# A recommender layer on one core: fields in five groups of four and three of two, and 22 weight loads halved

## The reference, cut to what matters

```python
sparse_embed = emb_tables[field_idx[None, :], x_sparse]      # 512 x 26 x 64
z = sparse_embed.reshape(B, N_FIELDS * K)
gram = jnp.einsum('bik,bjk->bij', sparse_embed, sparse_embed)
inner = gram[:, iu, ju]                                       # i < j
dnn_in = jnp.concatenate([x_dense, z, inner], axis=-1)        # 512 x 2002
h = jax.nn.relu(dnn_in @ w1 + b1)                             # w1: 2002 x 2002
out = jax.nn.sigmoid(h @ w2 + b2)
```

## Time and profile before

| | |
|---|---|
| median of the runs | 206.7 us |
| the profiled execution's own time | 207.33 us |
| its span, first to last instruction | 205.5 us |
| TensorE (PE) matmul, busy | 197.4 us (96%) |
| TensorE weight load (PEld), busy | 162.1 us |
| VectorE (DVE), busy | 145.1 us |
| ScalarE (ACT), busy | 129.9 us |
| GpSimd (POOL), busy | 125.0 us |
| mean granted TensorE clock | 0.988 of 2.4 GHz |

### The profile page before, as it was taken

One profiled execution on the slowest core, in us unless ns is written; L12 is line 12 of the kernel. 1 busy time (PEld: TensorE's weight loads), 2 busy tenths in 40 slices (PEclk: granted clock), 3 DMA queues, 4 the chain that ended last, 5 costly groups with the idle time before them and its releaser, 6 DMA issues.

```text
span 205.5 us, 3833 instructions
## 1 busy us (share of the span) xinstructions
PE 197.4 (96%) x1332; PEld 162.1 (79%) x1332; DVE 145.1 (71%) x342; ACT 129.9 (63%) x261; POOL 125.0 (61%) x169
## 2 busy tenths in 40 slices
PE   8994999999999999999999999999999999999993
PEld 8953888888888887887888888888888887788882
DVE  3574929696859769589874999688487787563573
ACT  2683627586958779687378755877699946632101
POOL 4777778778777783818988989889890000052000
PEclk9999799999999999999999999999999999999998
DMA  5579887676678589334599548988786185043000
GB/s 142 127 268 271 259 273 230 181 237 202 215 214 307 199 255 308 62 107 104 183 329 358 154 119 257 322 245 256 244 290 227 19 299 190 3 54 64 20 0 0
DMA packets 15206, 39.01 MB, mean 190 GB/s; under 512 B 3975, under 2 KB 5051, under 8 KB 15187
## 3 DMA queue, kind: packets, MB, share of 16 engines
q1 hardware_dynamic: 11250, 34.92, 52.1%
q0 software_dynamic: 3584, 3.76, 9.2%
q10 hardware_dynamic: 353, 0.08, 0.2%
HBM read 37.71 MB, written 0.69 MB: 187 GB/s over the span
## 4 chain that ended last, share of the span: by engine, by line
PE 85%; DVE 5%; POOL 4%; DMA 3%; issue 2%; ACT 0%; DVEq 0%
PE slot L1112 25%; PE slot L1115 24%; PE slot L1118 24%; PE slot L1072 5%; POOL E L843 4%; DMA E<-emb,row_idx 2%; PE slot L1102 2%; PE slot L1104 2%; PE slot L1103 2%; DVE w_lo L962 2%; DVE G L1010 1%; DMA x_idx<-idx 1%; DVE slot L1036 1%; DVE x_lo L992 0%; DVE T L979 0%
## 5 line engine op out<-in xcount | busy, mean ns | idle before, releaser
L843 POOL DMA_INDIRECT E<-emb,row_idx x104 | 110.9, 1067 | 33.3 <-issue 23.4
L962 DVE TENSOR_TENSOR w_lo<-w_raw,w_hi 128x500 fp32r<-128x500 f32 (+5 forms) x128 | 80.4, 671 | 11.8 <-ACT w_hi L880 11.6
L880 ACT CAST w_hi<-w_raw 128x1000 fp32r<-128x1000 f32 (+5 forms) x64 | 65.0, 1030 | 20.2 <-DMA w_raw<-w 11.8
L1112 PE MATMUL slot<-w_hi,x_hi 128*128 128x500 f32 (+5 forms) x236 | 74.9, 399 | 2.9 <-ACT x_hi L906 2.8
L1115 PE MATMUL slot<-w_lo,x_hi 128*128 128x500 f32 (+5 forms) x236 | 73.9, 394 | 0.1
L1118 PE MATMUL slot<-w_hi,x_lo 128*128 128x500 f32 (+5 forms) x236 | 73.1, 391 | 0.0
L1112 PEld LDWEIGHTS slot<-w_hi,x_hi 128*128 128x128 f32 (+2 forms) x236 | 43.9, 190 | 12.9 <-ACT x_hi L906 3.7
L1115 PEld LDWEIGHTS slot<-w_lo,x_hi 128*128 128x128 f32 (+2 forms) x236 | 45.0, 191 | 9.9 <-DVE w_lo L962 0.7
L1118 PEld LDWEIGHTS slot<-w_hi,x_lo 128*128 128x128 f32 (+2 forms) x236 | 44.9, 190 | 9.3
L911 ACT COPY ET<-T 32x128 f32<-32x128 f32 (+4 forms) x89 | 32.1, 360 | 2.1
L979 DVE STREAM_TRANSPOSE T<-E 128x256 f32<-128x256 f32 x24 | 10.6, 442 | 16.9 <-DMA E<-emb,row_idx 16.9
(11 more groups left out here) (42 smaller groups left out, 85.6 us busy)
## 6 DMA issues: line engine op xcount, KB each, us to landing
w_raw<-w SPq DMA_DIRECT2D x32, 501.0 KB, 4.8
w_raw<-w SPq DMA_DIRECT2D x32, 500.0 KB, 4.8
E<-emb,row_idx POOLq DMA_INDIRECT x104, 4.1
w_all<-w SPq DMA_DIRECT2D x1, 1001.0 KB, 4.5
gram_dram<-G SPq DMA_DIRECT2D x6, 84.5 KB
x_in<-gram_dram SPq DMA_DIRECT2D x6, 42.0 KB
x_in<-G SPq DMA_DIRECT2D x3, 58.5 KB
gram_dram<-G POOLq DMA_DIRECT2D x2, 84.5 KB, 5.3
```

Source lines behind the costliest of these rows:

```text
L843: nc.gpsimd.indirect_dma_start(out=E[:, k % ER, j, :], out_offset=None, in_=emb_rows, in_offset=bass.IndirectOffsetOnAxis(ap=row_idx[:, at ...
L880: nc.scalar.copy(w_parts(m)[0], w_source(m)).then_inc(w_hi_ready, 1)
L962: nc.vector.tensor_tensor(lo[:, cols], w_source(m)[:, cols], hi[:, cols].bitcast(F32), ALU.subtract)\
L1112: nc.tensor.matmul(acc[q], xh, hi[:, cols[q]], start=first, stop=False)
```

## The change

The 26 fields are now five groups of four (`WIDE`) and three of two (`NARROW`). In stage A the three narrow groups come first (`ORDER_A`), for batch tiles 0 and 1 in turn; in stage B they come last (`ORDER_B`). Each narrow group has its own place in X24; the intermediate T6 is shared by turns. Loads 4 to 25 (`HALVED`) are issued as two DMAs of 64 rows each, the first after gather `GATE[m]`, the second after gather `GATE[m] + 1`. `GATE` for m = 4, 5, 6 goes from 6, 7, 8 to 7, 9, 10. The two matmuls of `KEEP` are gone. `HELD_BACK` moves by one arrival, since two more arrivals come in A, and some assumed durations of the planner change.

```diff
-GROUP_GATHERS = [4] * WIDE + [2]
-GROUP_ORDER = [LAST] + list(range(WIDE))
+WIDE, NARROW = 5, 3
+GROUP_GATHERS = [4] * WIDE + [2] * NARROW
+ORDER_A = list(range(WIDE, GROUPS_Z)) + list(range(WIDE))
+ORDER_B = list(range(GROUPS_Z))
+ARRIVALS = ([(bt, g) for g in ORDER_A[:-2] for bt in (0, 1)] + [(bt, g) for bt in (0, 1) for g in ORDER_A[-2:]]
+            + [(bt, g) for g in ORDER_B for bt in (2, 3)])
...
-GATE = {2: 3, 3: 3, 4: 6, 5: 7, 6: 8, 7: 11, 8: 12, 9: 13, 10: 15, 11: 16, 12: 19, 13: 20, 14: 23, 15: 24, 16: 27, 17: 28,
+GATE = {2: 3, 3: 3, 4: 7, 5: 9, 6: 10, 7: 11, 8: 12, 9: 13, 10: 15, 11: 16, 12: 19, 13: 20, 14: 23, 15: 24, 16: 27, 17: 28,
         18: 31, 19: 32, 20: 35, 21: 36, 22: 39, 23: 40, 24: 41, 25: 43, 26: 50}
+HALVED = range(4, 26)
-KEEP_AT, KEEP = 3, 1
-HELD_BACK = {16: 2, 17: 4}
+HELD_BACK = {17: 2, 18: 4}
...
-ET_PARTS = [(LAST, LAST + 1), (0, 3), (3, 5), (5, 6)]
+ET_PARTS = [(WIDE, GROUPS_Z), (0, 2), (2, 4), (4, 5)]
...
-DVE_LEN = {"lo": 0.70, "turn": 0.46, "x24": 0.60, "x_lo": 0.44, "evac": 0.38, "park": 0.70, "drain": 0.86}
+DVE_LEN = {"lo": 0.70, "turn": 0.46, "x24": 0.50, "x_lo": 0.44, "evac": 0.38, "park": 0.70, "drain": 0.86}
-LAND = (1.7, 1.5, 1.1, 1.2) + (1.5,) * 10 + (4.5,)
+LAND = (1.7, 1.5, 1.5, 1.5) + (1.5,) * 12 + (4.5,)
...
-                    if m in GATE:
-                        sp.wait_ge(paced, paced_count(GATE[m]))
                     if m >= RAW:
                         sp.wait_ge(w_split, 2 * (m - RAW + 1))
-
-                    sp.dma_start(w_raw[:, m % RAW, 0:HALF_W[h]], w1[t, :, HALF_AT[h]:HALF_AT[h] + HALF_W[h]])\
-                      .then_inc(w_landed[m % RAW], 16)
+                    for n, rows in enumerate(load_rows(m)):
+                        if m in GATE:
+                            sp.wait_ge(paced, paced_count(GATE[m] + n))
+                        sp.dma_start(w_raw[rows, m % RAW, 0:HALF_W[h]], w1[t, rows, HALF_AT[h]:HALF_AT[h] + HALF_W[h]])\
+                          .then_inc(w_landed[m % RAW], 16)
...
+def load_rows(m):
+
+    return [slice(0, 64), slice(64, P)] if m in HALVED else [slice(0, P)]
...
             for step in PE_OPS:
-                if k == KEEP_AT and step[0] == "product":
-                    for n in range(KEEP):
-                        nc.tensor.matmul(slot[SLOT[cell_at(step)]][:, 0:BANK].rearrange("p (a b) -> p a b", a=4), ones[:],
-                                         ones[:].unsqueeze(1).to_broadcast([P, 4, P]), start=True, stop=True)
```

More of the change, by code:

```diff
@@ L159, in make_todo @@
     todo += [s for steps in later for s in steps[1:]]
-    first = [b_group("B1", 1, g) for g in GROUP_ORDER[:2]]
+    first = [b_group("B1", 1, g) for g in ORDER_B[:2]]
     todo += [s for bt in (2, 3) for f in first for s in f if s[2] == bt]
-    for n, g in enumerate(GROUP_ORDER[2:]):
+    for n, g in enumerate(ORDER_B[2:]):
         todo += b_group("B1", 1, g)
-        todo += b_group("B2", 0, GROUP_ORDER[n]) if n < 4 else []
-    rest = [s for g in GROUP_ORDER[4:] for s in b_group("B2", 0, g)]
+        todo += b_group("B2", 0, ORDER_B[n]) if n < 3 else []
+    rest = [s for s in b_group("B2", 0, ORDER_B[3])]
+    rest += [s for g in ORDER_B[4:] for s in b_group("B2", 0, g)]
+    todo, rest = todo + rest[:2], rest[2:]
     todo += mixed(rest[:7], gram({2, 3}), every=2) + rest[7:]
@@ L216, in length @@
         return 0.19 + 0.11 * n if engine == "act" else 0.16 + 0.11 * n
-    if op[0] in ("x_hi", "x_lo") and op[2] in [LAST] + INNER_KEYS:
+    if op[0] in ("x_hi", "x_lo") and op[2] >= WIDE:
         return 0.32
+    if op[0] == "turn" and ARRIVALS[op[1]][1] >= WIDE:
+        return 0.34
     if op[0] == "drain" and op[1][2] == "inner":
@@ L302, in et_ops @@
     def et_ops(bt, parts=range(len(ET_PARTS))):
-        return [("et", bt, p, i, h, v) for p in parts for i in range(2 if ET_PARTS[p][0] == LAST else 4) for h in (0, 1)
+        return [("et", bt, p, i, h, v) for p in parts for i in range(2 if ET_PARTS[p][0] == WIDE else 4) for h in (0, 1)
                 for v in ((0, 1) if bt in SPLIT else (None,))]
@@ L349, in update @@
             free = all_done(et_ops(bt - 2, [part_of(g)])) if bt >= 2 else 0.0
+            if g >= WIDE and (bt, g) in NARROWS[2:]:
+                back = NARROWS[NARROWS.index((bt, g)) - 2]
+                copied = all_done([("x24",) + back + (e,) for e in ("act", "dve")])
+                free = None if None in (free, copied) else max(free, copied)
             if free is not None:
@@ L443, in wanted @@
         if kind in ("turn", "x24", "x_hi", "x_lo"):
-            key = ARRIVALS[op[1]] if kind == "turn" else (op[1], LAST) if kind == "x24" else op[1:]
-            tail = {"turn": 2.1 if key[1] == LAST else 1.1, "x24": 1.3, "x_hi": 0.6, "x_lo": -0.3}[kind]
+            key = ARRIVALS[op[1]] if kind == "turn" else op[1:]
+            tail = {"turn": 1.7 if WIDE <= key[1] < IN_KEY else 1.1, "x24": 1.3, "x_hi": 0.6, "x_lo": -0.3}[kind]
             at = step_at(keys[key], tail)
@@ L484, in run @@
             if op + (other,) in done:
-                offer("act", ("x_hi", op[1], LAST), max(end, done[op + (other,)]) + HOP)
+                offer("act", ("x_hi",) + op[1:], max(end, done[op + (other,)]) + HOP)
         elif kind == "park":
@@ L490, in run @@
             bt, g = ARRIVALS[op[1]]
[L491 to L493 removed]
+            if g >= WIDE:
+                offer("act", ("x24", bt, g), end + HOP)
+                offer("dve", ("x24", bt, g), end + HOP)
             else:
@@ L594, in x_lo_count, with x24_count @@
     return X_LOS.index((bt, g)) + 1
+def x24_count(engine, bt, g):
+    return X24S[engine].index((bt, g)) + 1
 def turned_count(bt, g):
@@ L714, in x_group @@
             b = slice(bt * P, (bt + 1) * P)
-            if g == LAST:
-                return X24[:, bt % 2, :], x_hi[:, ZT - 1, b], x_lo[:, ZT - 1, b]
+            if g >= WIDE:
+                t = GROUP_TILES[g][0]
+                return X24[:, bt % 2, g - WIDE, :], x_hi[:, t, b], x_lo[:, t, b]
             return T[:, bt % 2, g], x_hi[:, 2 * g:2 * g + 2, b], x_lo[:, 2 * g:2 * g + 2, b]
@@ L876, in _ @@
                     m = op[1]
-                    act.wait_ge(w_landed[m % RAW], 16 * (m // RAW + 1))
+                    act.wait_ge(w_landed[m % RAW], sum(16 * len(load_rows(n)) for n in range(m % RAW, m + 1, RAW)))
                     if m >= HL:
@@ L1158 @@
                 w_rows[2 * g + h, Q * i:Q * i + Q] = DENSE + (4 * g + i) * K + Q * h + np.arange(Q)
-    for h in range(2):
-        for i in range(2):
-            at = 64 * h + Q * i
-            w_rows[ZT - 1, at:at + Q] = DENSE + (4 * WIDE + i) * K + Q * h + np.arange(Q)
+    for n in range(NARROW):
+        for h in range(2):
+            for i in range(2):
+                at = 64 * h + Q * i
+                w_rows[2 * WIDE + n, at:at + Q] = DENSE + (4 * WIDE + 2 * n + i) * K + Q * h + np.arange(Q)
     w_rows[NT - 1, 0:DENSE] = np.arange(DENSE)
```

73 lines of the change are left out of this document (36 added, 37 removed).

## The result

The change made the kernel slower: 210.85 us in the median of 13 runs (209.06 to 213.61), against 207.07 for the kernel before on the same chip (13 runs). The ratio is 1.0161, 95% interval 1.0133 to 1.0189. I had forecast 204.4, with 202.8 to 207.7 as the range: the sign is wrong, and the measured time lies outside the range.

A forecast was written before the change was run, and what follows sets the result against it. PE was taken to bound the kernel (85% of the chain); the thirteenth product 2.3 us earlier, other terms nothing, took the profiled 207.33 to 205.0, and the runs' 0.6 lower median gave 204.4 us, range 202.8 to 207.7.

The forecast's parts named there:

- the one on the halves: Loads 4 to 25 as 64-row DMAs: each piece completes one gather, 1.25 us, later, hidden by the late gather; no cost.
- the second rival: Halves do not help the gathers: gather 15 lands after 6.4 us as before, 0.8 gained, 205.9 us; chance 0.20.
- The landing of 4.9 us: Gather 15, issue to landing in the opening: 4.9 us, starting the thirteenth product at 29.7, against 32.00 before.
- The low clock: Rival, PE in the opening: about 2.4 us idle drops the clock again, price 1.8 us, 206.2 us; chance 0.24.
- both middle rivals: Clock falling again (0.24) and halves not helping gathers (0.20); together product thirteen 33.0 in effect, 1.0 us slower.
- the slower rival: DVE stands 3.9 us at a turn on PE's path and the clock falls too, 1.8: 210.1 us; chance 0.12.
- The cap on the gain: An earlier PE catches up with gathers 19, 27 and 31 in stage A, limiting the gain to 2.2 to 2.9 us.
- the grouping's 2.3: Narrow groups first in stage A: the thirteenth product starts 2.3 us earlier, and this goes through about whole.
- The price of 1.36 us per product: PE from the thirteenth product to the first gram: 32 products in 43.5 us, 1.36 us each.
- stage B's denser tail: Narrow groups last in stage B: 4.5 us more DVE work, inside 6.7 us of cover, costing nothing.
- The signs I had named for "wrong": Gather 15 landing over 6 us, clock 0.5 after 28 us, turn waiting over 2 us, or PE waits between 35 and 60.
- the ones: Removing two matmuls on ones before an idle stretch in PE's opening: 1.02 us of PE go, no gain or cost.

The follow-up runs named there:

- experiment 1: The changed kernel with loads 4 to 25 whole again (128 rows), grouping and gates kept: 207.08 us, ratio 1.0023.
- experiment 2: The kernel before with loads 4 to 25 as two 64-row halves, gates one gather apart, nothing else changed: 211.54 us, ratio 1.0207.
- experiment 4: The changed kernel with 64-row halves made of every other row instead of rows 0 to 63 and 64 to 127: 208.62 us, ratio 1.0064.
- experiment 10: The changed kernel with both row halves of a load bound to the same gather: 211.92 us, ratio 1.0223.
- experiment 3: The changed kernel with halves of all 128 rows and half the columns, same gates: 207.22 us, ratio 0.9977.
- experiment 5: The changed kernel with whole loads, and w2 and loads 26 to 30 held back to later gathers: 207.29 us, ratio 1.0007.
- experiment 12: The changed kernel with halves of all 128 rows and half the columns, measured once more unchanged: 206.99 us, ratio 0.9996.
- experiment 7: The changed kernel with 64-row halves for loads 4 to 9 only, whole loads from 10 on: 211.09 us, ratio 1.0173.
- experiment 9: The kernel before with loads 4 to 25 as two column halves of all 128 rows, bound to two gathers in turn: 206.64 us, ratio 0.9989.
- experiment 6: The kernel before with w2 and loads 26 to 30 held back to later gathers: 208.34 us, ratio 1.0055.

## Why the prediction was wrong, by its steps

**The step that failed is the one on the halves**: "So the halves cost nothing that the late gather does not hide. What they may bring is in the landing of the gathers." I had the rule that speaks against it, and put it in as the second rival, but priced it as "a half is as slow as a whole", so that gather 15 would land after 6.4 us as before, and gave it 0.20. Both are wrong. The price of a slower half is not its own duration, it is the queues' balance: two halves of 1.22 us each and 0.29 for the gathers are 2.73 us of work per 2.5 us. Part of it could have been worked out then, from the trace of the kernel before: the queues' share was 0.72, and loads are 0.57 of the time in the row of 40 to 60 us above; with them 1.5 times as dear the share is 0.72 + 0.57 × 0.5 = 1.0, and the queues are full for good. By the figures of the Trainium skill, SBUF — State Buffer, section on the DMA port swizzle (196 against 328 GB/s), an estimate would have been 1.67 times. The runs here show 1.6. The landing was 8.9 us, not 4.9, and outside the bounds 3.4 to 6.4, which came from queues that were not full. Experiments 1, 2, 4 and 10 show this.

**The landing of 4.9 us was too short even without row halves.** It was the median of three gathers, while the row of gather 15 itself had 6.4. With the new grouping and no row halves it took 5.3 to 6.8 us from issue to turn (experiments 1, 3, 4, 5 and 12); with row halves among loads 4 to 9 it took 8.3 to 9.5 (the kernel after and experiments 2, 7 and 10).

**The low clock** was priced at 1.8 us for about 2.4 idle. That 2.4 us are enough is shown by experiment 3, where PE stood 2.40 and the row of 25 to 30 us has a clock of 0.74. In the kernel after it followed on the late gather, after 4.69 idle, and cost 3.0 in the profiled execution. The range allowed for both middle rivals at once, but with a landing of 6.4 and 1.8 for the clock ("33.0 in effect"); with 8.9 and 3.0 the same sum gives product 13 at 33.7, 36.7 in effect, which is 4.7 slower: about 211.4, against 210.85 measured. The number of the slower rival, 210.1, came close to the result, and its condition (thirteenth product after 32.00) was met; but its mechanism, a w_lo behind a standing turn, was not what PE waited for. PE waited for the gather itself. The rival's mechanism occurs in experiment 3, at 2.4 us.

**The cap on the gain** failed as well, apart from the halves: I took 2.2 to 2.9 from gathers 19, 27 and 31, all ahead of the first gram. The binding place is behind it, the third gram, which needs the ET copies of the last gathers of stage A. In experiments 1 and 9 it waits and comes at 85.1 and 85.5, with first grams 1.7 and 2.0 us early. And where it came earlier (83.67 in experiment 5, 82.80 in 6) the lead went into small waits behind it. So the grouping's 2.3, which "goes through about whole", was 2.0 at product 13, 1.7 at the first gram, 0.5 at the third, and nothing in the median (1.0023, 0.9977 and 0.9996 in three measurements). With this cap in the sum the forecast would have been near "no change".

**A frame that misled:** the profile before shows one execution with 2.76 us of idle time and a low clock in the opening. In experiment 9, with the same grouping, the opening went by with a wait of 0.54 and clock 1.00, and its median is no better. Of the 29 executions beside it only 7 had a mean clock as low as the profiled one's. A loss seen in one execution was counted as one that all runs carry.

**What held.** The price of 1.36 us per product; twelve products done by 28.2 (28.56 measured); the step of 0.93 from landing to product (32.30 to 33.24, 0.94); gather 15's issue at 23.85 (23.41); with whole loads the thirteenth product at 29.7 (29.99, experiment 1), though in part by luck, as gather 15 was issued 0.55 earlier than assumed and took 0.85 longer to its turn; stage B's denser tail at nothing (4.12 at the fifth gram, 4.11 at the end). The signs I had named for "wrong" appeared: a landing over 6 us, a clock near 0.5 after 28 us, a turn waiting over 2 us with PE idle behind it. That the ones cost nothing was not tried by itself.

## What to carry to other kernels

If a load of all 128 partitions has to be split, split it by columns, which was free here, and not at partition 64: the same bytes on one half of the partitions took 1.6 times the queues' time. (Alternate rows kept the rate, but that version was 0.6% slower for a reason that stayed open.) Before more or slower DMAs are added, balance the queues over the period of the loop: work per period against the period, and if it is over one, as here, every landing in that stretch comes late, the gathers' too and not just those of the split loads. And follow a lead in PE's time to the next place that waits for something unchanged, past the first milestone: in experiment 1 it was worth 2.0, 1.7 and 0.5 us at three places in a row, and nothing in the median.

## What the hardware showed that I had not expected

- The share of the DMA engines was 1.00 to 1.06 while they moved 209 to 229 GB/s, and 0.85 to 1.02 in stretches in which they moved 302 to 352. The share alone does not tell the rate; the two must be read together.
- Halving 501 KB loads into 250 KB by columns was free: 312 GB/s against 331, with nearly twice the packets (2063 against 1058 in 20 us).
- Idle stretches of PE of 0.54 and 1.63 us left the granted clock at 1.00. After 2.40 (experiment 3) it was 0.74 on average from 25 to 30 us, after 2.76 (before) 0.57 for 3.9 us, and after 4.69 (after) 0.50 for six.
